# Perceiver layer with cross attention, heads and feed-forward: one block for the last two stages, and six fold pairs in two groups of three

## The chip, the cores and the metric

The kernel runs on one core of a Trainium2 chip. The metric is the device time of one execution in microseconds. Each kernel was run several times; the median counts, and one execution was also profiled.

## The reference

```python
x = x + _L0_xattn_ref(_layernorm(x), ctx_1024, gamma, beta, w_q, w_kv, w_out, b_out, gate)
x = x + _L0_attn_ref(_layernorm(x), W_Q, W_K, W_V)
x = x + _L0_ffn_ref(_layernorm(x), w_gate, w_up, w_down)
```

`x` is 64 x 32 x 512 (2048 tokens), the context 64 x 257 x 512, all float32. The cross attention normalises its input again with `gamma` and `beta`, has 16 heads of 64 elements, and gives `(out @ w_out + b_out) * tanh(gate)`. The second attention works inside each token: with Q, K, V split into 16 heads of 32 elements, K is softmaxed over the heads, Q over the elements, and the heads' products are mixed. The feed-forward has 1536 hidden elements, `silu(gate) * up`, and integer weights scaled by 1/127.

## The kernel before, in words

All large products are made three times over from a high and a low part of each operand (`three`, lines 80 to 84), with a moving side of 258 or 512 columns. The high parts come from ScalarE, the low parts (raw minus high) from VectorE or GpSimd.

There are three stages, each in a block of its own, so that each engine's program ends at the block's end and starts anew. `project_queries` writes the queries to memory. `cross_attention` works in 16 turns of four batches. `heads_and_mlp` makes output projection, second attention and feed-forward for 16 tiles of 128 tokens and then 4 turns of 512 tokens. Within a block the order of the instructions on each engine is written out by hand, and semaphores join the engines.

One turn of `cross_attention`, on TensorE: for each batch the probabilities are turned (`turn_probs`, line 574), the next batch is scored (`scores`), and the context is mixed by the probabilities in four chunks (`mix_chunk`, each 6 products). VectorE keeps each chunk (`keep_mix`, line 679). At the end of the turn `out_half` makes the heads' outputs in two halves (lines 600 and 607), ScalarE and VectorE split them into `x_o_hi` and `x_o_lo` (lines 794 and 701), and the sync queue stores them as `o_hi`, `o_lo` (line 423). Meanwhile the next turn's queries are folded with the key weights: `fold_pair` (line 540) makes eight matmuls of 64 rows for each of eight pairs of heads, ScalarE takes the high part (`high_fold`, line 780), VectorE the low part (`low_fold`, line 686). A pair uses two banks of PSUM (`FOLD_BANK`), and a pair that reuses banks waits until the earlier pair's low part is made (`FOLD_AFTER`): pair 3 for pair 0, pair 4 for pair 1, pair 5 for pair 2. VectorE's `keep_last` (lines 691 and 694) turns the last context row's probabilities; it waits for GpSimd's `last_ready`.

The last of the 16 turns is written out apart. It has no folds; instead the 20 pieces of the output and Q, K, V weights are loaded (`load_w`, line 434: 8 pieces of `w_out`, 4 each of `aq`, `ak`, `av`, 256 KB each), rounded by ScalarE (line 789) and split by GpSimd (even pieces) and VectorE (odd ones, `w_low`, line 394).

`heads_and_mlp` begins with four small loads and the loads of tiles 0 and 1 (`load`, lines 1061 and 1063: `a_oT_hi` and `a_oT_lo` of 512 KB each, `a_xin` of 256 KB), then six loads of feed-forward pieces (line 1089, 256 KB each). For each tile TensorE makes the output projection (24 products of `a_oT` with `w_out`, which lies in `w_cT` and the first part of `w_space`). VectorE adds gate, bias and input (`a_x`, line 1451) and takes moments and rows (`a_xn`, line 140, with GpSimd's power in between). TensorE turns them (line 1180), ScalarE and VectorE split them (`a_xT_hi`, `a_xT_lo`, lines 1326 and 1440), and then come the K, Q and V projections of 12 products each. A tile's output projection stands one tile ahead: that of tile 1 stands between tile 0's turning and its K projection.

Of the kernel before, what the change touches and what calls it, by code (L numbers as in the profile page):

```python
# [13 lines left out]

# [8 lines left out]
P = 128  # L23
# [299 lines left out]
def cross_attention(nc, hw, ahead, ctx_nat, ctx_T, last_T, q_dram, v_dram, o_hi, o_lo, identity, heads):  # L323
# [17 lines left out]
    with ExitStack() as ctx:  # L341
        s = Scope(nc, ctx, "x")
        wk, w_v, q, raw_n, raw_T = ahead.wk, ahead.w_v, ahead.q, ahead.raw_n, ahead.raw_T
        fold = hw.fold
        mix = s.sb("mix", [P, DC, GB, heads * SQ])
        cn = [s.pair(f"cn{i}", [P, KT, dim]) for i in range(2)]
        cT = hw.cT
        prob = s.sb("prob", [P, TILES, SKE])
        pT = [s.pair(f"pT{i}", [P, KT, heads * SQ]) for i in range(2)]
        last_p = s.sb("last_p", [P, TILES, GB, SQ])  # L350
        last_v = s.sb("last_v", [P, inner])
        last_z, last_t = s.sb("last_z", [P, TILES, SQ]), s.sb("last_t", [P, TILES, SQ])
# [24 lines left out]
        last_kept = s.count("last_kept", 1)
        mixed, mix_kept = s.count("mixed", GB * DC), s.count("mix_kept", GB * DC)
        o_ready = s.count("o_ready", 2, 2)
        o_hi_done, o_lo_done = s.count("o_hi_done", 2), s.count("o_lo_done", 2, 2)  # L380
        o_stored = s.count("o_stored", 64, 32)
        l_loaded, v_ready, v_copied, v_stored = s.sem("l_loaded"), s.sem("v_ready"), s.sem("v_copied"), s.sem("v_stored")
        all_last, lT = mix[0:B, 0, 0:2, :], mix[:, 1, 0, 0:DC * B].rearrange("p (c b) -> p c b", c=DC)
        slots = [wk[:, j, :] for j in range(PAIRS)]
        slots += [a[:, :, :].rearrange("p j n -> p (j n)")[:, h * dim:(h + 1) * dim] for a in (q, raw_T) for h in range(2)]
        RING, PIECES = len(slots), len(hw.pieces)
        w_loaded = [s.sem(f"w_loaded{i}") for i in range(RING)]
        w_hi_done, w_lo_done = s.sem("w_hi_done"), [s.sem("w_lo_pool"), s.sem("w_lo_dve")]
# [12 lines left out]
        @block.sync
        def _(sp):
            def load_T(t, b):
                sp.dma_start(raw_T[:, :, :], ctx_T[t * GB + b].rearrange("(c p) k -> p c k", p=P)).then_inc(T_loaded.sem, 16)

            def load_n(t, b):
                sp.dma_start(raw_n[:, :, :], ctx_nat[t * GB + b, 0:KT * P, :].rearrange("(k p) d -> p k d", p=P))\
                    .then_inc(n_loaded.sem, 16)

            def load_q(t, ahead):  # L410
                sp.dma_start(q[:, :, :], q_dram[:, :, bass.ds((t + ahead) * P, P)]).then_inc(q_loaded.sem, 16)

            def load_v(t):
                sp.wait_ge(o_ready.sem, o_ready.at(t, 0))
                for g in range(HT):
                    dst = last_v[g * SQ:g * SQ + GB, :].rearrange("b (i g e) -> b i g e", g=HT, e=HE)[:, :, g, :]
                    src = v_dram[bass.ds(t * GB, GB), :].rearrange("b (i g e) -> b i g e", g=HT, e=HE)[:, :, g, :]
                    sp.dma_start(dst, src).then_inc(v_loaded.sem, 16)

            def store_out(t, m):  # L420
                sp.wait_ge(o_lo_done.sem, o_lo_done.at(t, m + 1))
                for dst, src in zip((o_hi, o_lo), o):
                    sp.dma_start(dst[4 * m:4 * m + 4, :, bass.ds(t * P, P)].rearrange("j p n -> p j n"), f32(src[:, :, :]))\
                        .then_inc(o_stored.sem, 16)

            def load_w(numbers):
                for n in numbers:
                    if n == 0:
                        sp.wait_ge(fold_ready.sem, fold_ready.at(TURNS - 1, PAIRS))
                    if n == PAIRS + 2:  # L430
                        sp.wait_ge(Tlo_done.sem, Tlo_done.at(TURNS - 1, GB))
                    if n >= RING:
                        sp.wait_ge(w_lo_done[n % 2], (n - RING) // 2 + 1)
                    sp.dma_start(slots[n % RING], hw.pieces[n][0]).then_inc(w_loaded[n % RING], 16)

            def turn(t, more):
                load_v(t)
                if not more:
                    load_w(range(PAIRS + 2))
                if more:  # L440
                    sp.wait_ge(fold_ready.sem, fold_ready.at(t, PAIRS))
                    load_q(t, 1)
                for b in range(GB - 1):
                    if b + 2 < GB or more:
                        sp.wait_ge(nlo_done.sem, nlo_done.at(t, b + 2))
                        load_n(t, b + 2)
                    if more:
                        sp.wait_ge(Tlo_done.sem, Tlo_done.at(t, b + 4))
                        load_T(t, b + 4)
                if not more:  # L450
                    load_w(range(PAIRS + 2, RING + 4))
                store_out(t, 0)
                if more:
                    sp.wait_ge(nlo_done.sem, nlo_done.at(t, GB + 1))
                    load_n(t, GB + 1)
                    sp.wait_ge(Tlo_done.sem, Tlo_done.at(t, GB + 3))
                    load_T(t, GB + 3)
                else:
                    load_w(range(RING + 4, PIECES))
                store_out(t, 1)  # L460

            sp.dma_start(ident[:, :], identity).then_inc(once, 16)
            sp.dma_start(lT, last_T.rearrange("(c p) b -> p c b", p=P)).then_inc(l_loaded, 16)
            for done in (T_loaded, q_loaded, n_loaded):
                sp.sem_inc(done.sem, 16)  # L465
            for g in range(HT):
                sp.dma_start(own[g * SQ:(g + 1) * SQ, :], identity[0:SQ, 0:GB]).then_inc(once, 16)
            sp.wait_ge(cleared, 1)
            for b in range(2):
                sp.wait_ge(Tlo_done.sem, Tlo_done.at(0, b + 1))  # L470
                load_T(0, b + 1)
# [5 lines left out]
            with sp.Fori(0, TURNS - 1) as t:  # L477
                turn(t, True)
# [1175 lines left out]
```

## Time and profile before

| | |
|---|---|
| median of 3 runs | 1916.24 us (1915.59 to 1916.68) |
| the profiled execution, its own time | 1916.39 us |
| its span in the profile | 1914.6 us |
| TensorE matmul busy | 97% of the span |
| VectorE, ScalarE, GpSimd busy | 54%, 35%, 29% |
| mean granted clock of TensorE | 0.991 of 2.4 GHz |
| a turn of the cross attention | 66.87 us |
| start of the last cross turn, end of the cross attention on TensorE | about 1154 us, 1208.97 us |

The span begins with the first instruction of the program and ends with the last; the execution's own time has 1.8 us more around it. The profile names lines of the kernel, tiles by the names in the program (`x_` for the cross attention, `a_` for heads, `f` for feed-forward, `w_` and `e_` for what both share), and for each instruction what ended the idle time in front of it. PE is TensorE, PEld its weight loads, DVE VectorE, ACT ScalarE, POOL GpSimd, SPq the sync queue's issues.

### The profile page before, as it was taken

How to read it: one execution, taken by the hardware profiler on the slowest of the kernel's cores; microseconds unless marked ns; L12 is line 12 of the kernel's file. 1: busy time of each engine (PE TensorE's matmuls, PEld its weight loads, DVE VectorE, ACT ScalarE, POOL GpSimd, SP SyncE). 2: the span in 40 equal slices, each digit the busy share in tenths (PEclk: the TensorE clock that was granted, in tenths of full speed). 3: DMA queues.
4: the chain of work that ended last, by engine and by line, in shares of the span. 5: the costliest groups of instructions: out<-in, count | busy, mean ns of one | idle time of the engine just before them, and what ended most of it. 6: DMA issues, size and time to landing. Idle time of an engine off the chain costs nothing. (4 is left out here: it accounts for less than half of the span.)

```text
span 1914.6 us, 36622 instructions
## 1 busy us (share of the span) xinstructions
PE 1857.1 (97%) x14096; PEld 1607.2 (84%) x14096; DVE 1039.1 (54%) x2015; ACT 666.2 (35%) x1356; POOL 558.6 (29%) x546
## 2 busy tenths in 40 slices
PE   5989999999999999999999999599999999999999
PEld 4868988988998898899989888488888788888887
DVE  7614555455455545545554555388889763333322
ACT  3235444444444444444444445221111231111111
POOL 3015334433533444353344436231112000000000
PEclk9999999999999999999999999799999999999999
DMA  7323223322322332232233223633352131000000
GB/s 244 128 85 99 86 61 103 99 77 77 110 78 66 99 99 78 76 110 77 67 98 99 81 73 127 184 84 88 99 154 73 57 126 65 3 34 32 21 24 22
DMA packets 166629, 165.65 MB, mean 87 GB/s; under 512 B 8688, under 2 KB 123888, under 8 KB 166576
## 3 DMA queue, kind: packets, MB, share of 16 engines
q1 hardware_dynamic: 162144, 156.27, 27.1%
q10 hardware_dynamic: 4432, 8.65, 1.2%
q8 instruction: 36, 0.59, 0.1%
q14 instruction: 17, 0.14, 0.0%
HBM read 131.08 MB, written 33.82 MB: 86 GB/s over the span
## 5 line engine op out<-in xcount | busy, mean ns | idle before, releaser
L497 POOL TENSOR_TENSOR x_prob<-x_prob,x_share 128x256 f32<-128x256 f32 x256 | 157.0, 613 | 602.9 <-DVE x_share L662 595.7
L82 PE MATMUL x_ps<-w_cT_hi,w_space_hi 128*128 128x258 f32 x1024 | 296.1, 289 | 0.0
L83 PE MATMUL x_ps<-w_cT_lo,w_space_hi 128*128 128x258 f32 x1024 | 290.7, 284 | 0.0
L84 PE MATMUL x_ps<-w_cT_hi,w_space_lo 128*128 128x258 f32 x1024 | 288.5, 282 | 0.0
L679 DVE COPY x_mix<-x_ps 128x512 f32<-128x512 f32 x256 | 176.2, 688 | 115.1 <-PE x_ps L84 114.9
L82 PE MATMUL x_ps<-x_pT_hi,x_cn_hi 128*128 128x512 f32 x512 | 208.1, 406 | 1.5 <-DVE x_mix L679 1.5
L686 DVE TENSOR_TENSOR w_space_lo<-x_ps,w_space_hi 128x512 fp32r<-128x512 f32 x256 | 161.0, 680 | 78.4 <-ACT w_space_hi L780 45.8
L84 PE MATMUL x_ps<-x_pT_hi,x_cn_lo 128*128 128x512 f32 x512 | 201.2, 393 | 0.0
L769 ACT ACTIVATE x_prob<-x_ps,x_negmax 128x257 f32<-128x257 f32 x256 | 122.1, 477 | 227.1 <-DVE x_negmax L657 227.1
L83 PE MATMUL x_ps<-x_pT_lo,x_cn_hi 128*128 128x512 f32 x512 | 199.7, 390 | 0.0
L657 DVE TENSOR_REDUCE x_negmax<-x_ps 128x1 f32<-128x257 f32 x256 | 108.1, 422 | 166.2 <-PE x_ps L84 166.2
L82 PEld LDWEIGHTS x_ps<-w_cT_hi,w_space_hi 128*128 128x128 f32 x1024 | 193.8, 189 | 2.0 <-issue 0.2
L83 PEld LDWEIGHTS x_ps<-w_cT_lo,w_space_hi 128*128 128x128 f32 x1024 | 193.8, 189 | 0.0
L84 PEld LDWEIGHTS x_ps<-w_cT_hi,w_space_lo 128*128 128x128 f32 x1024 | 193.5, 189 | 0.0
L780 ACT ACTIVATE w_space_hi<-x_ps 128x512 fp32r<-128x512 f32 x256 | 132.4, 604 | 124.0 <-PE x_ps L540 124.0
L491 POOL TENSOR_TENSOR x_cn_lo<-e_raw_n,x_cn_hi 128x1024 fp32r<-128x1024 f32 x64 | 153.3, 2395 | 0.0
L540 PEld LDWEIGHTS x_ps<-e_q,e_wk 64*128 64x128 f32 x2048 | 122.2, 192 | 27.7 <-issue 18.7
L486 POOL TENSOR_TENSOR w_cT_lo<-e_raw_T,w_cT_hi 128x1028 fp32r<-128x1028 f32 x64 | 141.5, 2210 | 5.8 <-ACT w_cT_hi L757 5.8
L540 PE MATMUL x_ps<-e_q,e_wk 64*128 64x128 f32 x2048 | 134.4, 282 | 7.5 <-SPq L465 4.9
L600 PE MATMUL x_ps<-x_mix,e_wv 128*64 128x128 f32 x2048 | 138.3, 275 | 0.8 <-DVE x_mix L679 0.8
L600 PEld LDWEIGHTS x_ps<-x_mix,e_wv 128*64 128x64 f32 x2048 | 114.2, 137 | 12.3 <-issue 5.4
L82 PEld LDWEIGHTS x_ps<-x_pT_hi,x_cn_hi 128*128 128x128 f32 x512 | 96.1, 188 | 23.6 <-DVE x_mix L679 1.9
(205 smaller groups left out, 3546.6 us busy)
## 6 DMA issues: line engine op xcount, KB each, us to landing
e_raw_T<-ctx_T SPq DMA_DIRECT2D x64, 514.0 KB, 4.0
e_raw_n<-ctx_nat SPq DMA_DIRECT2D x64, 512.0 KB, 3.6
q<-q_q ACTq DMA_DIRECT2D x16, 512.0 KB, 2.8
e_q<-q SPq DMA_DIRECT2D x16, 512.0 KB, 4.2
o_hi<-x_o_hi SPq DMA_DIRECT2D x32, 256.0 KB, 2.4
o_lo<-x_o_lo SPq DMA_DIRECT2D x32, 256.0 KB, 3.0
a_oT_hi<-o_hi SPq DMA_DIRECT2D x16, 512.0 KB, 4.4
a_oT_lo<-o_lo SPq DMA_DIRECT2D x16, 512.0 KB, 5.6
```

Of the source, the lines that this page charges most:

```text
L82: pe.matmul(out, lhs[0], rhs[0], start=start, stop=False)
L83: pe.matmul(out, lhs[0], rhs[1], start=False, stop=False)
L84: return pe.matmul(out, lhs[1], rhs[0], start=False, stop=stop)
L486: pool.tensor_tensor(cT[b % 2][1][:, :, 0:SK], raw_T[:, :, :], f32(cT[b % 2][0][:, :, 0:SK]), ALU.subtract).then_inc(Tlo_done.sem, 1)
L491: pool.tensor_tensor(cn[b % 2][1][:, :, :], raw_n[:, :, :], f32(cn[b % 2][0][:, :, :]), ALU.subtract).then_inc(nlo_done.sem, 1)
L497: pool.tensor_tensor(prob[:, i, 0:KT * P], prob[:, i, 0:KT * P], share[:, i:i + 1].to_broadcast([P, KT * P]), ALU.mult)\
L540: mm = pe.matmul(ps[:, FOLD_BANK[j][h], c * P:(c + 1) * P], wk[r, j, c * P:(c + 1) * P], q[r, j, :], start=True, stop=True)
L600: pe.matmul(out[h], w_v[:, c, n * HE:(n + 1) * HE], mix[:, c, :, n * SQ:(n + 1) * SQ], start=c == 0, stop=False)
L679: dve.tensor_copy(mix[:, c, b, :], ps[:, M_BANK[c % 2], :]).then_inc(mix_kept.sem, 1)
L686: dve.tensor_tensor(lo, ps[:, FOLD_BANK[j][h], :].rearrange("p (c n) -> p c n", n=SQ), f32(hi), ALU.subtract).then_inc(fold_lo.sem, 1)
L769: act.activation(prob[:, i, 0:SK], ps[:, S_BANK[i], 0:SK], ACT.Exp, bias=negmax[:, i:i + 1], accum_out=total[:, i:i + 1]).then_inc(exp_don ...
L780: act.activation(of_head(fold[0], 2 * j + h), ps[:, FOLD_BANK[j][h], :].rearrange("p (c n) -> p c n", n=SQ), ACT.Copy)\
```

## The change

The last two stages become one block: `cross_attention` and `heads_and_mlp` return their programs for each engine, and `build` puts them one behind the other. PSUM and the identity are shared. The tiles of the heads are laid out anew, so that tile 0's and tile 1's inputs, bias, gate and mask can be loaded while the cross attention still runs. In the last cross turn the sync queue loads tile 0 after three quarters of the mixing, tile 1 after the pieces of `ak`, then mask, bias and gate; ScalarE's `tanh`, VectorE's gated bias and GpSimd's first two additions also move there. The output projection of tile 1 now stands ahead of tile 0's turning, in another bank (`DOTS`). GpSimd and VectorE each make two of the last weight splits later. The feed-forward's first loads wait for all weight splits. Tile 1's projection no longer stands ahead of K.

In the turns with folds, pairs 0 to 2 stand together ahead of the last batch's mixing, pairs 3 to 5 between its second and third chunk.

The core of the diff, without the changed indentation:

```diff
     def tensor(pe):
@@ turn
                 mix_chunk(t, 2, 2)
                 mix_chunk(t, 2, 3)
                 if more:
-                    fold_pair(t, 1, 0)
-                    fold_pair(t, 1, 1)
+                pe.wait_ge(pT_lo.sem, pT_lo.at(t, GB * KT))
+                for j in range(3):
+                    fold_pair(t, 1, j)
                 for c in range(DC):
                     mix_chunk(t, 3, c)
-                    if more and c % 2 == 0:
-                        fold_pair(t, 1, 2 + c)
-                        fold_pair(t, 1, 3 + c)
+                if more and c == 1:
+                    for j in range(3, 6):
+                        fold_pair(t, 1, j)
     def vector(dve, first_bias):
                 keep_mix(t, 2, 2)
-                if more:
-                    low_fold(t, 1, 0)
                 keep_mix(t, 2, 3)
                 if more:
+                low_fold(t, 1, 0)
                     low_fold(t, 1, 1)
                 for c in range(DC):
                     keep_mix(t, 3, c)
                     if c == 0:
                         keep_last(t)
-                    if more and c > 0:
-                        low_fold(t, 1, 1 + c)
+                if more and c < 2:
+                    low_fold(t, 1, 2 + c)
...
                 if more:
+                low_fold(t, 1, 4)
                     low_fold(t, 1, 5)
...
                 low_out(t, 1)
                 if not more:
-                    w_low(dve, range(15, PIECES, 2))
+                first_bias()
+                w_low(dve, (15,))
     def sync(sp, first_loads):
-                    load_w(range(PAIRS + 2, RING + 4))
+                load_w(range(PAIRS + 2, RING))
+                first_loads(0)
+                load_w(range(RING, RING + 4))
+                first_loads(1)
                 store_out(t, 0)
...
-            sp.wait_ge(o_stored.sem, 32 + TURNS * o_stored.per)
     def gpsimd(pool, first_bias):
-                    w_low(pool, range(0, PIECES, 2))
+                w_low(pool, range(0, 16, 2))
+                first_bias()
+                w_low(pool, range(16, PIECES, 2))
     def scalar(act, first_tanh):
                     w_high(range(RING, 16))
+                first_tanh()
                 high_out(t, 1)
...
+    def late_weights(dve):
+        w_low(dve, range(17, PIECES, 2))
@@ heads_and_mlp
+    def first_loads(sp, part):
+
+        c, last = cross, cross.last
+        if part == 0:
+            sp.wait_ge(c.mixed.sem, c.mixed.at(last, 3 * c.mixed.per // c.batches))
+            sp.wait_ge(c.turned.sem, c.turned.at(last, c.turned.per))
+            sp.wait_ge(c.last_ready.sem, c.last_ready.at(last, c.batches))
+        sp.wait_ge(c.o_stored.sem, c.o_stored.at(part + 1, 0))
+        load(sp, 0, part)
+        if part == 1:
+            sp.wait_ge(c.mixed.sem, c.mixed.at(last, c.mixed.per))
+            for dst, src in ((mask[:, :], same_token), (gated_bias[:, :], bias.partition_broadcast(P)),
+                             (gate_b[:, :], gate.partition_broadcast(P))):
+                sp.dma_start(dst, src).then_inc(once, 16)
...
@@ sync, step
+                if tile_of(t, i) == 0:
+                    sp.wait_ge(cross.o_stored.sem, cross.o_stored.at(cross.last + 1, 0))
+                load(sp, t, i + 2)
@@ sync, load_w of the feed-forward
                 for n in numbers:
+                if n == 0:
+                    for done in cross.w_lo_done:
+                        sp.wait_ge(done, len(hw.pieces) // 2)
...
+                if n == gate_up_at[1] + 4:
+                    sp.wait_ge(x2_stored[0].sem, x2_stored[0].at(TURNS, 0))
@@ gpsimd
+    def first_rows(pool):
+        pool.wait_ge(bias_done, 1)
+        add_bias(pool, 0, 0)
+        add_bias(pool, 0, 1)
@@ tensor, step
+            if tile_of(t, i) == 0:
+                add_out(t, 1, DOTS)
                 if there(t, i):
                     pe.wait_ge(normed.sem, normed.at(t, i + 1))
...
-                if there(t, i + 1):
+            if there(t, i + 1) and tile_of(t, i) != 0:
...
+                if tile_of(t, i) == 0:
+                    weights_done(16)
                     project(t, i, 1, K, k_ready)
...
+        def weights_done(pieces):
+            for done in cross.w_lo_done:
+                pe.wait_ge(done, pieces // 2)
...
-            pe.wait_ge(once, 64)
+        weights_done(PAIRS)
             all_steps(pe, step)
@@ vector, step
                     norm_scale(dve, xn, src, moments, rstd, 1).then_inc(normed.sem, 1)
+                if tile_of(t, n) == 0:
+                    cross.late_weights(dve)
```

GpSimd's program of the heads still begins with `pool.sem_inc(x2_done.sem, 4)`, the four credits for which VectorE waits ahead of each `a_x`; it now stands behind the last weight splits. The heads' tiles `a_oT`, `a_x`, `a_xin` have new places, and with them the feed-forward's `y`, `h` and their helpers.

How the instructions move is seen in three places. TensorE, at the end of a turn with folds; `e_q,e_wk` are the fold matmuls, `x_pT,x_cn` the mixing. Before, for the islands of pairs 2 and 3 and of pairs 4 and 5:

```order
L540 MATMUL x_ps<-e_q,e_wk 128x128 x16
...
L540 MATMUL x_ps<-e_q,e_wk 128x128 x8
L536 REGISTER_ALU
L540 MATMUL x_ps<-e_q,e_wk 128x128 x8
L82 MATMUL x_ps<-x_pT_hi,x_cn_hi 128x512
...
L536 REGISTER_ALU
L540 MATMUL x_ps<-e_q,e_wk 128x128 x8
```

Now, the first island of three and the second:

```order
L622 REGISTER_ALU
L532 REGISTER_ALU
L538 MATMUL s_ps<-e_q,e_wk 128x128 x24
L585 REGISTER_ALU
L83 MATMUL s_ps<-x_pT_hi,x_cn_hi 128x512
...
L534 REGISTER_ALU
L538 MATMUL s_ps<-e_q,e_wk 128x128 x8
L534 REGISTER_ALU
L538 MATMUL s_ps<-e_q,e_wk 128x128 x8
L534 REGISTER_ALU
L538 MATMUL s_ps<-e_q,e_wk 128x128 x8
```

Pairs 0 to 2 have one row of 24 matmuls, and pairs 3, 4 and 5 follow each other with a wait ahead of each.

The sync queue, from the last pieces of `aq` in the last cross turn. Before:

```order
L434 DMA e_raw_T<-aq 128x512 x2
L434 DMA e_wk<-ak 128x512 x4
L423 DMA o_hi<-x_o_hi 128x4x128
L423 DMA o_lo<-x_o_lo 128x4x128
L434 DMA e_wk<-av 128x512 x4
```

Now:

```order
L430 DMA e_raw_T<-aq 128x512 x2
L1082 DMA a_oT_hi<-o_hi 128x8x128
L1082 DMA a_oT_lo<-o_lo 128x8x128
L1084 DMA a_xin_1062<-x 128x512
L430 DMA e_wk<-ak 128x512 x4
...
L1084 DMA a_xin_1063<-x 128x512
L1077 DMA a_mask<-same_token 128x128
L1077 DMA a_bias<-b_out 128x512
L1077 DMA a_gate<-gate 128x1
L419 DMA o_hi<-x_o_hi 128x4x128
```

Tile 0's three loads stand ahead of `ak`, tile 1's and the small ones between `ak` and the first store.

GpSimd, from its last weight splits on. Before:

```order
L394 TENSOR_TENSOR w_space_lo<-e_wk,w_space_hi 128x512 x4
L341 UNCONDITIONAL_BRANCH
...
L1159 MEMSET a_power 128x4
L1127 TENSOR_TENSOR a_xin_3424<-a_xin_3424,a_bias 128x512
L1132 TENSOR_TENSOR a_rstd<-a_shifted,a_power 128x1
```

Now:

```order
L391 TENSOR_TENSOR w_space_lo<-e_wk,w_space_hi 128x512 x2
L1149 TENSOR_TENSOR a_xin_1062<-a_xin_1062,a_bias 128x512
L1149 TENSOR_TENSOR a_xin_1063<-a_xin_1063,a_bias 128x512
L391 TENSOR_TENSOR w_space_lo<-e_wk,w_space_hi 128x512 x2
L1187 MEMSET a_power 128x4
L1160 TENSOR_TENSOR a_rstd<-a_shifted,a_power 128x1 x2
```

Two additions stand between the splits, and the last two splits ahead of the first power.

## Rows read from the trace of the kernel before

**Rows 1.** The page: busy time, share of the span, instructions of each engine.

```profile
PE 1857.1 (97%) x14096; PEld 1607.2 (84%) x14096; DVE 1039.1 (54%) x2015; ACT 666.2 (35%) x1356; POOL 558.6 (29%) x546
```

**Rows 2.** Waits of TensorE, 1190 to 1300: engine line, released by, us, times, longest.

```profile
PE a_ps L82 <- DMA a_xin<-x: 15.6, 1, 15.6
PE a_ps L1180 <- DVE a_xn L140: 4.1, 1, 4.1
```

**Rows 3.** Windows: us, busy of PE, PEld, DVE, ACT, POOL, PEclk, DMA share, GB/s.

```profile
1194.00:1198.00 4.00, 2.53 (x11) 1.76 (x11) 3.96 (x5) 2.15 (x5) 4.00 (x4) 1.00 0.06 8
1226.00:1230.00 4.00, 4.00 (x12) 3.14 (x11) 0.00 (x0) 0.00 (x0) 0.00 (x0) 0.56 1.10 356
```

**Rows 4.** Timeline of TensorE at the boundary: start, us, operation, [idle before, releaser].

```profile
1208.58 0.39 PE L607 MATMUL x_ps<-x_last_p,x_last_v 128*64 128x128 f32 x4
1224.52 0.77 PE L82 MATMUL a_ps<-w_cT_hi,a_oT_hi 128*128 128x512 f32 x1 [15.55 <-DMA a_xin<-x]
...
1225.51 0.63 PE L84 MATMUL a_ps<-w_cT_hi,a_oT_lo 128*128 128x512 f32 x1
1225.94 0.63 PE L82 MATMUL a_ps<-w_cT_hi,a_oT_hi 128*128 128x512 f32 x1
...
1244.11 0.39 PE L82 MATMUL a_ps<-w_space_hi,a_xT_hi 128*128 128x512 f32 x1
...
1252.28 0.60 PE L1180 MATMUL a_ps<-a_ident,a_xn 128*128 128x128 f32 x4
```

**Rows 5.** Timeline of TensorE around two fold islands of the eighth turn.

```profile
589.48 0.40 PE L84 MATMUL x_ps<-x_pT_hi,x_cn_lo 128*128 128x512 f32 x1
589.81 2.06 PE L540 MATMUL x_ps<-e_q,e_wk 64*128 64x128 f32 x32
...
592.13 0.39 PE L83 MATMUL x_ps<-x_pT_lo,x_cn_hi 128*128 128x512 f32 x1
...
596.63 0.39 PE L84 MATMUL x_ps<-x_pT_hi,x_cn_lo 128*128 128x512 f32 x1
```

**Rows 6.** Timeline of VectorE in the same stretch.

```profile
587.67 1.29 DVE L674 TENSOR_TENSOR x_pT_lo<-x_ps,x_pT_hi 128x512 fp32r<-128x512 f32 x2 [0.70 <-ACT x_pT_hi L775]
...
594.64 0.68 DVE L679 COPY x_mix<-x_ps 128x512 f32<-128x512 f32 x1
...
595.67 0.69 DVE L694 TENSOR_TENSOR x_last_p<-x_last_t,x_own 128x512 f32<-128x512 f32 x1
597.06 0.69 DVE L679 COPY x_mix<-x_ps 128x512 f32<-128x512 f32 x1 [0.70 <-PE x_ps L84]
597.67 1.28 DVE L686 TENSOR_TENSOR w_space_lo<-x_ps,w_space_hi 128x512 fp32r<-128x512 f32 x2
```

**Rows 7.** Timeline of the sync queue's issues at the boundary.

```profile
1191.90 6.77 SPq L434 DMA_DIRECT2D e_wk<-ak  x4
...
1224.27 1.86 SPq L1089 DMA_DIRECT2D f_raw<-wg  x4
```

**Rows 8.** DMA issues of 1185 to 1240: KB each, median us to landing.

```profile
a_xin<-x SPq DMA_DIRECT2D x3, 256.0 KB, 6.3
```

**Rows 9.** Timeline of VectorE and GpSimd at the boundary.

```profile
1210.84 0.68 DVE L394 TENSOR_TENSOR w_space_lo<-e_wk,w_space_hi 128x512 fp32r<-128x512 f32 x1
1211.22 3.10 POOL L394 TENSOR_TENSOR w_space_lo<-e_wk,w_space_hi 128x512 fp32r<-128x512 f32 x2 [2.41 <-ACT w_space_hi L789]
...
1220.62 0.48 DVE L1569 TENSOR_SCALAR a_bias<-a_bias,a_tanh 128x512 f32<-128x512 f32 x1 [5.76 <-ACT a_tanh L1386]
...
1224.55 1.27 POOL L1127 TENSOR_TENSOR a_xin<-a_xin,a_bias 128x512 f32<-128x512 f32 x1 [9.06 <-DMA a_xin<-x]
...
1232.58 0.75 DVE L1451 SCALAR_TENSOR_TENSOR a_x<-a_ps,a_tanh,a_xin 128x512 f32<-128x512 f32 x1 [11.47 <-PE a_ps L84]
...
1235.14 1.48 DVE L140 TENSOR_SCALAR a_xn<-a_x,a_moments,a_rstd 128x512 f32<-128x512 f32 x1 [0.67 <-POOL a_rstd L1132]
...
1253.54 0.69 DVE L1440 TENSOR_TENSOR a_xT_lo<-a_ps,a_xT_hi 128x512 fp32r<-128x512 f32 x1 [0.35 <-ACT a_xT_hi L1326]
```

More of the change, by code:

```diff
@@ L13 @@
 from contextlib import ExitStack
+from dataclasses import dataclass
 import concourse.bass as bass
@@ new lines, in cross_attention @@
+    s = Scope(nc, ctx, "x")
+    wk, w_v, q, raw_n, raw_T = ahead.wk, ahead.w_v, ahead.q, ahead.raw_n, ahead.raw_T
+    fold = hw.fold
+    mix = s.sb("mix", [P, DC, GB, heads * SQ])
+    cn = [s.pair(f"cn{i}", [P, KT, dim]) for i in range(2)]
+    cT = hw.cT
+    prob = s.sb("prob", [P, TILES, SKE])
+    pT = [s.pair(f"pT{i}", [P, KT, heads * SQ]) for i in range(2)]
+    last_p = s.sb("last_p", [P, TILES, GB, SQ])
+    last_v = s.sb("last_v", [P, inner])
+    last_z, last_t = s.sb("last_z", [P, TILES, SQ]), s.sb("last_t", [P, TILES, SQ])
@@ L912, in pair, with heads_and_mlp @@
         return self.sb(name + "_hi", shape, F32R), self.sb(name + "_lo", shape, F32R)
-def heads_and_mlp(nc, ahead, hw, x, bias, gate, o_hi, o_lo, x2, identity, same_token, wg, wu, wd, out, scale):
+def heads_and_mlp(nc, ctx, ps, ident, start, cross, ahead, hw, x, bias, gate, o_hi, o_lo, x2, identity, same_token, wg, wu, wd, out, scale):
     tokens, dim = x.shape
@@ new lines, in heads_and_mlp @@
+    x2o = [area.sb("x2o0", [P, dim])]
+    over = area.at
+    oT = [None, area.pair("oT1", [P, PAIRS, P])]
+    on_oT = [Area(nc, "f1", over), None]
+    on_y = Area(nc, "fy", area.at)
+    x1 = [area.sb(f"x1{i}", [P, dim]) for i in range(4)]
+    xin = [area.sb(f"xin{i}", [P, dim]) for i in range(2)]
+    area.at += 64
+    on_oT[1] = Area(nc, "f0", area.at)
+    oT[0] = area.pair("oT0", [P, PAIRS, P])
+    gated_bias = area.sb("bias", [P, dim])
+    x2o.append(area.sb("x2o1", [P, dim]))
+    mask = area.sb("mask", [P, P])
@@ new lines, in heads_and_mlp, with gate_up_pieces @@
+    w_g.append(on_rows.pair("wg2", [P, DC, dim]))
+    w_u.append(on_rows.pair("wu2", [P, DC, dim]))
+    assert on_rows.at == over and HC == 12 and CHUNKS == 3
+    wsrc = [w.rearrange("(c p) n -> c p n", p=P) for w in (wg, wu, wd)]
+    pieces, gate_up_at, down_at = [], [], []
+    def gate_up_pieces(n):
+        for src, dst in ((wsrc[0], w_g), (wsrc[1], w_u)):
+            pieces.extend((src[c, :, n * dim:(n + 1) * dim], dst[n][0][:, c, :], dst[n][1][:, c, :]) for c in range(DC))
+        gate_up_at.append(len(pieces))
```

2035 lines of the change are left out of this document (1018 added, 1017 removed).

## The prediction

> **What bounds the kernel now.** I read the page first. TensorE is busy for 1857.1 of 1914.6 us [rows 1], so a change can only pay where TensorE waits or where its stream has dead steps. The waits of TensorE around the end of the cross attention come next [rows 2]: 15.6 us until the first tile's `a_xin` has landed, and 4.1 us until its normalised rows `a_xn` exist. The windows [rows 3] give the clock: 1.00 of full speed (2.4 GHz) in the last cross turn, but 0.56 at 1226 to 1230, where the first products of the heads run after the long wait; a good part of that window is at the lower level (1.2 GHz). The timeline places this [rows 4]: the last product of the cross attention begins its group at 1208.58 and is over at 1208.97, the first head product begins at 1224.52, the K projection of tile 0 at 1244.11. Everything from 1208.97 to 1244.11 is 35.1 us for 48 output products and four transposes.
>
> What a product costs at full clock is in the same rows: K, Q and V of tile 0 are 36 products between 1244.11 and 1252.28, so 0.227 us each. 48 of them are 10.9 us.
>
> The second place is the fold islands. In every turn but the last, eight pairs of 64-row products (`L540`) stand between groups of other products. The timeline of one of them [rows 5]: the last product before an island starts at 589.48, the island at 589.81, and the second product after it at 592.13, 2.65 us in all. The 16 matmuls in it (32 records) take 2.06 - 0.27 = 1.79 us from first to last start, 0.112 each, and two ordinary steps of 0.23 make 0.46. The remaining **0.40 us** is what entering and leaving one island costs.
>
> **The change, part by part.**
>
> *Islands.* Pairs 0 to 5 stood in three islands of two, now in two of three; pairs 6 and 7 stay. One entry and exit less in 15 turns (the last turn has no folds): 15 x 0.40 = **6.0 us less**, if no new wait appears. Two could. (a) The new wait for `pT_lo` before pair 0: its work on VectorE begins at 587.67 and lasts 1.29 us [rows 6], over at 588.96; the island begins at 589.81 [rows 5]. 0.85 us to spare, cost nothing. (b) Pair 5 waits for VectorE's subtractions of pair 2, and these now stand behind `keep_mix(3,0)` and `keep_last`. Count from the first island's start. The last matmul of three pairs starts at 24 x 0.112 = 2.68, the second product behind an island 0.53 later (592.13 against 589.81 + 1.79), the sixth four steps of 0.23 later, at 4.14, and the copy follows 0.43 later, as 597.06 follows 596.63 [rows 5, 6]: 4.57. From that copy to `x_last_p` are 1.03 us (594.64 to 595.67), the next instruction can start 0.60 behind it, and the two subtractions take 1.28 [rows 6]: done at 7.48. TensorE comes to pair 5 at 4.14 + 6 x 0.23 + 0.32 + 16 x 0.112 + 0.1 = 7.73, and loads its weights about 0.1 earlier. About 0.1 us to spare. Price zero, bound from above one VectorE step (0.60) in each turn.
>
> *The boundary.* Both blocks become one, so no branch, no barrier and no wait for the last stores stand between them. The loads of tile 0 and tile 1 move ahead of the weights `ak` and of the last stores on the sync queue. Tile 0 goes out after three quarters of the last turn's mixing, about 1191.8, just ahead of the four `ak` loads that now begin at 1191.90 [rows 7]; a load behind two others takes 6.3 us to land [rows 8], so it is there near 1199, ten microseconds early. Tile 1 goes out after the `ak` loads, whose issues end at 1191.90 + 6.77 = 1198.67 [rows 7]; two more issues, and 6.3 us: near 1206. Two tiles are 2.5 MB, in a stretch of which the queue spent most waiting for VectorE. Behind them stand mask, bias and gate, which by the same count land near 1208, and the first store. ScalarE's `tanh` waits for the gate ahead of the second `x_o_hi`, and so does VectorE's slot at 1210.84 behind the second `x_o_lo` [rows 9]: 2.8 us to spare, less ScalarE's and VectorE's own 1.3. I take zero, bound 1 us, since the chain below starts there.
>
> TensorE then goes from 1208.97 straight into 48 products: 10.9 us and about 0.4 for the step between kinds, done at 1220.3. Beside it runs the chain to tile 0's rows. VectorE's slot is at 1210.84, and the bias takes 0.48 there: 1211.32. GpSimd adds it to two tiles at 1.27 each: 1213.86. It then makes two more weight splits of the same size (I take 1.27 each, as for the addition), and only after them hands out the four credits for which VectorE's first `a_x` waits: 1216.4. From `a_x` to the end of `a_xn` took 1235.14 + 1.48 - 1232.58 = 4.04 us: 1220.5 [rows 9]. So the transposes start at 1220.5 or 1220.6, both sides equal. Before, the second 24 products covered the time from the transposes to K; now they are used up. Transposes, ScalarE's copy and VectorE's difference took 1253.54 + 0.69 - 1252.28 = 1.95 us, with the release 2.0 [rows 4, 9]: **this wait is new, some 1.7 us of idle TensorE**. K starts at 1222.6 where it started at 1244.11: **21.5 us less**. Ends of this term: 1220.3 + 2.0, if GpSimd is earlier, gives 21.8; with the slower splits (3.10 for two [rows 9]) it is 20.9.
>
> On the two splits the Trainium skill (SBUF — State Buffer, the rule on the shared port pair) says that a VectorE instruction with two SBUF inputs and a GpSimd instruction that reads SBUF exclude each other, the later one blocking fully. By that rule the VectorE split that now follows the bias at 1211.4 meets GpSimd's first addition, which would begin some 0.7 us later, and the K projection with it: 20.8 instead of 21.5, a sum of 1890.5. It lies inside the ends just named (20.9 within 0.1).
>
> *What is late next.* The six feed-forward loads moved behind the last of the weight splits, the two that VectorE makes after `a_xn`: 1220.5 + 1.3 = 1221.8. Six issues at 1.86 / 4 are 2.8 us, then come the three loads of tile 2, whose last goes out about 1.2 later and lands 6.3 us after that [rows 7, 8]: 1232.1. TensorE wants it 8.2 + 0.3 us after K's start: 1231.1. **1.0 us of new wait**; I take 0.9. Ends: 0 if the loads run without gaps, 2.5 if ScalarE's first feed-forward pieces and GpSimd's third addition, both now late, push more.
>
> Sum, against the profiled execution's own 1916.39 (span 1914.6): -21.5 - 6.0 + 0.9 = -26.6, **1889.8 us**. The median of the runs shown is 0.15 lower than that execution, which I leave.
>
> **The rivals.**
> 1. *Pair 5 stops every turn.* For it speaks the margin of 0.1 us, against it that the trace's VectorE steps repeat to 10 ns. If VectorE is one step of 0.60 late, 0.5 us are lost 15 times: 1889.8 + 7.5 = 1897.3. Chance 0.10.
> 2. *The boundary keeps part of its gap.* A chain that is late (gate, GpSimd, tile 2) by 3 us in all, for instance: 1893. Nor is the lower clock excluded: TensorE idles about 1.7 us before K. In 1194 to 1198 TensorE was busy for 2.53 of 4.00 us and the clock stayed at 1.00 [rows 3], while products at 1225.51 and 1225.94, behind the wait of 15.6 us, are 0.43 apart [rows 4]. If it fell, I count 12 products at 0.43 instead of 0.227, as many as the window at 0.56 holds: 2.4 us more, 1892. [...] Chance of this rival 0.15.
> 3. *It ends slower.* The mechanism would be the island of three: `keep_last` waits for GpSimd's `x_last_z`, and now holds back pair 2's subtractions and so pair 5. If it made TensorE wait more than 26.6 / 15 = 1.8 us a turn beyond what the island saves, the kernel would be slower; at 2.2 us it is 1896 + 27, some 1923. Against it: VectorE went from that copy to `x_last_p` in 1.03 us without a wait [rows 6]. Chance 0.03.
> 4. *It does not do what it says:* tile 0 is held by the mixing or by the stores, and the gap stays, leaving the 6 us of the folds: 1910. Chance 0.02.
>
> **How the numbers follow.** The forecast has 0.70. Its own range is 1887.5 (margins better than worked out, no wait for tile 2) to 1892. Rival 2 adds up to 1894.5; what is left out above is rival 1, 3 and 4 with some 0.15. So 1887.5 to 1894.5. A measurement can tell about 0.2% (3.8 us) from no change; the first two cases and the forecast lie beyond it: faster 0.95, same 0.02, slower 0.03.
>
> **What would show it.** Right: the wait for `a_xin` of 15.6 us gone, K of tile 0 within 14 us of the last cross product, a wait of 1.5 to 2 us ahead of it that ends with `a_xT_lo`, one of about 1 us for tile 2's load, the clock at 1.00 throughout, and turns that are 0.40 us shorter, with no wait inside the islands. Wrong: a wait on `w_space_lo` in each turn (rival 1), products 0.43 us apart after the boundary, or a wait for `a_xin` of more than 3 us.

## The result and the profile after

The changed kernel took 1898.82 us (median of 4 runs, 1897.20 to 1899.87), the kernel before beside it on the same chip 1916.46 (1915.59 to 1919.39, 4 runs). The ratio is 0.9905, 95% interval 0.9887 to 0.9922. It is faster, by 17.6 us instead of the 26.6 that the sum gave, and outside the range of 1887.5 to 1894.5.

The profiled execution took 1897.99 us, its span is 1896.2. The row of the engines hardly differs from [rows 1]; TensorE is busy 98% of the span where it was 97%:

```profile
PE 1857.4 (98%) x14096; PEld 1604.4 (85%) x14096; DVE 1039.5 (55%) x2015; ACT 664.8 (35%) x1356; POOL 559.2 (29%) x546
```

**The boundary came as summed.** TensorE's waits between 1180 and 1300, which answer to [rows 2]; the columns are the same:

```profile
PE s_ps L83 <- DVE x_mix L677: 1.5, 1, 1.5
PE s_ps L83 <- DVE a_xT_lo L1481: 1.4, 1, 1.4
PE s_ps L598 <- DVE x_mix L677: 0.8, 1, 0.8
PE s_ps L83 <- DMA a_xin<-x: 0.4, 1, 0.4
```

Its timeline there, which answers to [rows 4]:

```profile
1201.75 0.39 PE L605 MATMUL s_ps<-x_last_p,x_last_v 128*64 128x128 f32 x4
1202.07 0.50 PE L83 MATMUL s_ps<-w_cT_hi,a_oT_hi 128*128 128x512 f32 x1
...
1215.30 0.50 PE L83 MATMUL s_ps<-w_space_hi,a_xT_hi 128*128 128x512 f32 x1 [1.41 <-DVE a_xT_lo L1481]
...
1223.60 0.60 PE L1207 MATMUL s_ps<-s_ident,a_xn 128*128 128x128 f32 x4
1224.56 0.47 PE L83 MATMUL s_ps<-w_cT_hi,a_oT_hi 128*128 128x512 f32 x1 [0.36 <-DMA a_xin<-x]
```

The waits of 15.6 and 4.1 us are gone; the two that end with `x_mix` stood in the kernel before as well, with the same lengths. From the last cross product to K of tile 0 it is 13.5 us (1201.75 to 1215.30), with one wait for `a_xT_lo` in it, and tile 2's load costs 0.4. K begins 28.81 us earlier than it did (1244.11, [rows 4]).

**The islands came as summed, too.** TensorE's timeline in the eighth turn, which answers to [rows 5]:

```profile
586.73 0.40 PE L85 MATMUL s_ps<-x_pT_hi,x_cn_lo 128*128 128x512 f32 x1
587.05 2.95 PE L538 MATMUL s_ps<-e_q,e_wk 64*128 64x128 f32 x48
589.93 0.50 PE L83 MATMUL s_ps<-x_pT_hi,x_cn_hi 128*128 128x512 f32 x1
...
592.57 0.39 PE L85 MATMUL s_ps<-x_pT_hi,x_cn_lo 128*128 128x512 f32 x1
592.89 2.95 PE L538 MATMUL s_ps<-e_q,e_wk 64*128 64x128 f32 x48
```

Both islands hold three pairs (48 records), and neither they nor the products behind them show a wait in brackets. The second one is as long as the first (2.95 us), so nothing stopped between its pairs either. From one turn's first product with `x_last_p` to the next it is 66.41 us where it was 66.85 (mean of 14 turns each).

**What was gained is lost again in the feed-forward.** The first row transposes of its second and third turn, before:

```profile
1608.62 0.60 PE L1251 MATMUL a_ps<-a_ident,a_m_xn 128*128 128x128 f32 x4
...
1708.59 0.49 PE L1251 MATMUL a_ps<-a_ident,a_m_xn 128*128 128x128 f32 x3
```

and after:

```profile
1582.93 0.60 PE L1287 MATMUL s_ps<-s_ident,a_m_xn 128*128 128x128 f32 x4
...
1685.30 0.60 PE L1287 MATMUL s_ps<-s_ident,a_m_xn 128*128 128x128 f32 x4
```

A turn takes 102.37 us instead of 99.97. The lead of the changed kernel is 27.6 us when the feed-forward starts (1498.6 against 1471.1, unrounded), 25.7 after its first turn, 23.3 and 20.9 after the next two, 18.4 at the end: **9.2 us go there**. No wait does it. Windows of one such turn (us; busy and count of PE, PEld, DVE, ACT, POOL; clock; DMA share; GB/s), before:

```profile
1608.00:1708.00 100.00, 100.00 (x450) 82.78 (x449) 34.46 (x59) 16.95 (x28) 1.01 (x1) 1.00 0.09 32
```

and after:

```profile
1583.00:1685.00 102.00, 102.00 (x448) 82.53 (x447) 34.52 (x58) 16.94 (x28) 1.01 (x1) 1.00 0.09 31
```

TensorE is busy throughout, at the same clock of 1.00 (2.4 GHz), beside the same work of the other engines and the same DMA traffic, and still needs 2% longer for as many products. Groups of the same products by shape (name, count, busy us, mean ns of one record), before:

```profile
L82 PE MATMUL a_ps<-a_m_xT_hi,f_wg_hi 128*128 128x512 f32 x16 | 6.3, 396 | 0.0
L83 PE MATMUL a_ps<-a_m_xT_lo,fhi_wg 128*128 128x512 f32 x16 | 6.2, 389 | 0.0
L84 PE MATMUL a_ps<-a_m_xT_hi,flo_wg 128*128 128x512 f32 x16 | 6.2, 389 | 0.0
L82 PE MATMUL a_ps<-ft_wd_hi,fo_h_hi 128*128 128x512 f32 x16 | 6.2, 390 | 0.0
```

and after:

```profile
L83 PE MATMUL s_ps<-a_m_xT_hi,f_wg_hi 128*128 128x512 f32 x16 | 6.4, 399 | 0.0
L84 PE MATMUL s_ps<-a_m_xT_lo,fhi_wg 128*128 128x512 f32 x16 | 6.3, 395 | 0.0
L85 PE MATMUL s_ps<-a_m_xT_hi,flo_wg 128*128 128x512 f32 x16 | 6.3, 395 | 0.0
L83 PE MATMUL s_ps<-ft_wd_hi,f_h_hi 128*128 128x512 f32 x16 | 6.3, 395 | 0.0
```

Every group is 3 to 6 ns longer. A record overlaps its neighbours, so the pace is better read from the starts. Ten products further it is 2.27 us before:

```profile
1649.65 0.39 PE L83 MATMUL a_ps<-ft_wd_lo,fo_h_hi 128*128 128x512 f32 x1
...
1651.92 0.39 PE L84 MATMUL a_ps<-a_m_xT_hi,flo_wg 128*128 128x512 f32 x1
```

and 2.32 us after:

```profile
1623.62 0.39 PE L85 MATMUL s_ps<-a_m_xT_hi,flo_wu 128*128 128x512 f32 x1
...
1625.94 0.39 PE L83 MATMUL s_ps<-ft_wd_hi,f_h_hi 128*128 128x512 f32 x1
```

Over the last two turns (intervals of 218 to 250 ns between two starts, nearly 900 of them) the products stood 226.7 to 229.0 ns apart before and 232.6 to 233.1 after, by group. On average that is 5.6 ns, and 432 products of a turn by 5.6 ns are 2.4 us, the whole loss.

What differs? The instructions are the same in the same order. Some operands have moved: `m_xT`, the moving operand of gate and up (512 columns), `h`, the stationary operand of down, and the weights `wg2` and `wu2`, these by 24064 bytes, which is a multiple of 256. The weights are stationary in gate and up and moving in down. The first bytes in a partition, and the remainder by 256:

| tile | before | after |
|---|---|---|
| `m_xT` (hi) | 211392, 192 | 211776, 64 |
| `h` (first, hi) | 141760, 192 | 189440, 0 |
| `wg0`, `wu0` | 8320, 128 (`wg0`) | the same |
| other `wg`, `wu`, all `wd` | 192 | 192 |

Before, all but `wg0` and `wu0` stood at 192, and the products with just these two were the slower ones, at 229.0. That is the theory of the experiments: **a product's pace hangs on where its two operands lie.** The rival is the merged program: instructions that lie elsewhere, or something that the other engines do beside. Paces below are means by group over the last two feed-forward turns of the profiled execution; with another choice of intervals they move by up to 0.4 ns.

### The profile page after: what moved, and what is told of

Read it like the earlier page. It is cut to its first block, busy times and chain, and to the rows that moved or that the text cites. A ratio compares the mean times of both kernels' runs of the same rounds, so it can differ in the third digit from the quotient of the medians.

```text
span 1896.2 us, 36612 instructions
## 1 busy us (share of the span) xinstructions
PE 1857.4 (98%) x14096; PEld 1604.4 (85%) x14096; DVE 1039.5 (55%) x2015; ACT 664.8 (35%) x1356; POOL 559.2 (29%) x546
## 4 chain that ended last, share of the span: by engine, by line
PE 90%; DVE 1%; DMA 1%; SPq 1%; POOL 0%; issue 0%; ACT 0%; ACTq 0%; DVEq 0%; POOLq 0%
PE s_ps L83 24%; PE s_ps L84 23%; PE s_ps L85 23%; PE s_ps L538 7%; PE s_ps L598 6%; PE s_ps L572 3%; PE s_ps L605 1%; PE s_ps L1265 1%; PE s_ps L1276 1%; PE s_ps L1207 0%; DMA a_xin<-x 0%; DMA a_m_xn<-x 0%; PE s_ps L1287 0%; PE s_ps L546 0%; PE s_ps L1256 0%
## 5 line engine op out<-in xcount | busy, mean ns | idle before, releaser
L83 PE MATMUL s_ps<-w_cT_hi,w_space_hi 128*128 128x258 f32 x1024 | 295.9, 289 | 0.0
L84 PE MATMUL s_ps<-w_cT_lo,w_space_hi 128*128 128x258 f32 x1024 | 290.5, 284 | 0.0
L85 PE MATMUL s_ps<-w_cT_hi,w_space_lo 128*128 128x258 f32 x1024 | 288.4, 282 | 0.0
L677 DVE COPY x_mix<-s_ps 128x512 f32<-128x512 f32 x256 | 176.7, 690 | 121.7 <-PE s_ps L85 121.7
L83 PE MATMUL s_ps<-x_pT_hi,x_cn_hi 128*128 128x512 f32 x512 | 206.4, 403 | 1.5 <-DVE x_mix L677 1.5
L767 ACT ACTIVATE x_prob<-s_ps,x_negmax 128x257 f32<-128x257 f32 x256 | 122.2, 477 | 226.7 <-DVE x_negmax L655 226.6
L85 PE MATMUL s_ps<-x_pT_hi,x_cn_lo 128*128 128x512 f32 x512 | 201.0, 393 | 0.0
L84 PE MATMUL s_ps<-x_pT_lo,x_cn_hi 128*128 128x512 f32 x512 | 199.8, 390 | 0.0
L83 PEld LDWEIGHTS s_ps<-w_cT_hi,w_space_hi 128*128 128x128 f32 x1024 | 193.7, 189 | 2.0 <-issue 0.2
L84 PEld LDWEIGHTS s_ps<-w_cT_lo,w_space_hi 128*128 128x128 f32 x1024 | 193.9, 189 | 0.0
L85 PEld LDWEIGHTS s_ps<-w_cT_hi,w_space_lo 128*128 128x128 f32 x1024 | 193.3, 189 | 0.0
```

Of the source, the lines that this page charges most:

```text
L83: pe.matmul(out, lhs[0], rhs[0], start=start, stop=False)
L84: pe.matmul(out, lhs[0], rhs[1], start=False, stop=False)
L85: return pe.matmul(out, lhs[1], rhs[0], start=False, stop=stop)
L677: dve.tensor_copy(mix[:, c, b, :], ps[:, M_BANK[c % 2], :]).then_inc(mix_kept.sem, 1)
L767: act.activation(prob[:, i, 0:SK], ps[:, S_BANK[i], 0:SK], ACT.Exp, bias=negmax[:, i:i + 1], accum_out=total[:, i:i + 1]).then_inc(exp_don ...
```

## The experiments

Each number beside a label is a median of 4 to 5 runs; the kernel before took 1918.40, 1917.82 and 1917.66 us beside the three groups of runs.

**1. Both operands back to 192, nothing else.**

```diff
-    on_oT[1] = Area(nc, "f0", area.at)
+    on_oT[1] = Area(nc, "f0", area.at + 192)
-    m_xn, m_xT = area.sb("m_xn", [P, TT, dim]), area.pair("m_xT", [P, DC, N])
+    m_xn = area.sb("m_xn", [P, TT, dim])
+    area.at += 128
+    m_xT = area.pair("m_xT", [P, DC, N])
```

> The changed kernel with two tiles moved and no instruction changed: m_xT 128 bytes further (its offset within 256 bytes is 192 again, as in the kernel before) and the pair h 192 bytes further (192 again). Theory 'places': the products of the feed-forward became slower because of where their operands lie. Then the products go from 232.8 ns apart back to 227, a feed-forward turn from 102.4 to 100.0 us, and the time falls by about 9 us to 1889.5. Rival 'program': the slower products come from the merged block (where the instructions lie and how they are fetched), or from something that ACT, DVE or the queues do beside them; then a turn stays at 102.4 us and the time at 1898.8.

1890.19 us, ratio 0.9855 (0.9839 to 0.9872). One feed-forward turn and one group of it:

```profile
1582.00:1682.00 100.00, 100.00 (x451) 82.87 (x450) 34.52 (x58) 16.98 (x29) 1.01 (x1) 1.00 0.10 32
```

```profile
L84 PE MATMUL s_ps<-a_m_xT_lo,fhi_wg 128*128 128x512 f32 x16 | 6.2, 389 | 0.0
```

The turn is back at 99.95 us, the pace at 226.7 (229.0 with `wg0` and `wu0`). The rival falls: the merged block with the same instructions is as fast as the old one.

**2. Each of the two alone.** Only the second half of the edit, then only the first.

> The changed kernel with m_xT alone 128 bytes further. Places: the gate and up products (288 of the 432 of a turn, 6.3 ns each for two thirds of them and 4 ns for the third with wg0 and wu0) get back to their old pace, the down products stay at 232.6 ns: 6.4 us less than the changed kernel, 1892.4. Program: 1898.8.

1893.69 us, a turn 101.07 us, gate and up at 227.7, down at 233.2.

> The changed kernel with the pair h alone 192 bytes further. Places: the down products (144 of a turn, 5.8 ns each, four turns) get back to 226.8 ns, gate and up stay slow: 3.3 us less than the changed kernel, 1895.5. Program: 1898.8.

1897.09 us, a turn 101.79 us, gate and up at 233.0, down at 228.5. From 102.37 the two take 1.30 and 0.58 us off a turn, together 1.88 of 2.42: the last half microsecond comes only with both, since a group whose operands are well placed is slower beside slow groups than in experiment 1 (228.5 and 227.7 instead of 226.9 and 226.7). The expectations left that out: they had 1.6 and 0.8 us less a turn, 1.30 and 0.58 came. In four turns this is 1.2 and 1.0 us of the 1.3 and 1.6 by which the two times lie above them.

**3. The same displacement in the kernel before,** whose `m_xT` then stands at 64.

```diff
-        m_xn, m_xT = area.sb("m_xn", [P, TT, dim]), area.pair("m_xT", [P, DC, N])
+        m_xn = area.sb("m_xn", [P, TT, dim])
+        area.at += 128
+        m_xT = area.pair("m_xT", [P, DC, N])
```

> The kernel before with m_xT 128 bytes further, so that its offset within 256 bytes is 64, as in the changed kernel; nothing else. Places: gate and up products go from 227 to 233 ns, a turn from 100.0 to 101.6 us, the time to 1922.9 (6.4 us more). Program: no change, 1916.5.

1924.80 us, 6.4 us above the kernel before (ratio 1.0035, 1.0021 to 1.0049), a turn 101.84 us (101.6 expected), gate and up at 233.0, and down, which has both its operands where they were, at 228.8 instead of 226.9. One displaced operand makes the old program slower, with no change in its instructions.

**4. Distance, or one good place?** Experiment 1 with other numbers:

```diff
-    on_oT[1] = Area(nc, "f0", area.at + 192)
+    on_oT[1] = Area(nc, "f0", area.at + 64)
-    area.at += 128
+    area.at += 64
```

> The changed kernel with m_xT 64 and h 64 bytes further. Offsets within 256 bytes are now 128 for m_xT (the operand that moves through in gate and up), 128 for wg0 and wu0, 192 for the other gate and up weights; 64 for h (the stationary operand of down) against 192 for wd. Theory 'distance' (what counts is the stationary operand's offset less that of the moving one: 0 gave 226.7 ns, 192 gave 229.0, 64 and 128 gave 232.6 to 233.2): products with wg0 and wu0 at 226.7 ns, all other gate and up ones at 233, down at 233; time 1890.2 - 0.9 + 4.8 + 3.4 = 1897.5. Rival 'one good place' (an operand is fast at offset 192 and slow elsewhere, each by itself): products with wg0 and wu0 stay at 229 or slower, 233 for the rest; time 1898.8 or more.

1895.94 us, 1.6 below the expectation; the time alone would not tell the two theories apart, the groups do. Three groups of its feed-forward:

```profile
L84 PE MATMUL s_ps<-a_m_xT_lo,fhi_wg 128*128 128x512 f32 x16 | 6.3, 394 | 0.0
L85 PE MATMUL s_ps<-a_m_xT_hi,fr_wg_lo 128*128 128x512 f32 x16 | 6.3, 394 | 0.0
...
L84 PE MATMUL s_ps<-a_m_xT_lo,f_wg_hi 128*128 128x512 f32 x16 | 6.2, 389 | 0.0
```

The order has turned round: `wg0` at 128, which was the slower one wherever the others were fast, is now the fast one (227.7 ns apart), since `m_xT` stands at 128 as well; those at 192 take 233.2, down 232.0.

Then `area.at += 192` ahead of `m_xT` and `area.at + 128` for `h`, which puts `m_xT` at 0 and `h` at 128:

> The changed kernel with m_xT 192 and h 128 bytes further: offsets 0 for m_xT, 128 for h. Distance: wg0 and wu0 are 128 away (233 ns), the other gate and up weights 192 away (229 ns), h against wd 192 away (229 ns); time 1890.2 + 1.6 + 1.8 + 1.2 = 1894.8. One good place: nothing but slow products, 1898.8.

1894.22 us: `wg0` and `wu0` 232.4, the other gate and up 229.6, down 229.7. So it is the distance, the stationary operand's place less that of the moving one. The feed-forward products of these runs together:

| distance in 256 bytes | ns from start to start | from |
|---|---|---|
| 0 | 226.7 to 227.0; 227.7 to 228.8 beside slow groups | before, experiments 1 to 5 |
| 64 | 232.6 to 233.2 | after (`wg0`, `wu0`, down), experiment 4 (other gate and up) |
| 128 | 232.0 to 233.0 | after (other gate and up), experiment 4 (down; `wg0`, `wu0`) |
| 192 | 229.0 to 229.7 | before, experiment 4 |

The period is not more than 256: 211392 and 61632 (`wg1`) are an odd multiple of 256 apart and fast. Distances that are no multiple of 64 were not tried, and why the distance matters stays open.

**5. The same for the rest.** Experiment 1, and:

```diff
+    on_ahead.at += 64
     w_g, w_u = [on_ahead.pair("wg0", [P, DC, dim])], [on_ahead.pair("wu0", [P, DC, dim])]
```

> places_both with wg0, wu0 and the six raw tiles behind them 64 bytes further too, so that wg0 and wu0 stand at 192 as m_xT does. Distance: their 96 products a turn go from 229.0 to 226.7 ns, four turns: 0.9 us less than places_both, 1889.3. If what is left at 229 ns has another cause: 1890.2.

1889.07 us; `wg0` and `wu0` at 226.9, a turn 99.72. The 0.23 us a turn are there, 0.9 in all.

Then also the mixing of the cross attention and `oT0` (the line ahead of `m_xT` becomes 192, and `h` lies where `oT0` does):

```diff
+    s.sb("gap", [P, 48])
     pT = [s.pair(f"pT{i}", [P, KT, heads * SQ]) for i in range(2)]
...
-    area.at += 64
+    area.at += 256
     on_oT[1] = Area(nc, "f0", area.at)
```

> both_and_wg0, and a gap of 192 bytes ahead of the cross attention's pT (with everything behind it in the cross attention) and ahead of oT0, so that pT stands at 192 as cn does, and oT0 as the wo pieces that lie in the space tiles. Distance: the 1536 products of pT and cn go from 229 to 226.7 ns (3.5 us in all) and those of oT0 in eight of the heads' tiles from 232.6 towards 227 (about 1.1 us): 1884.7. If the cross attention's turns do not follow their products (a wait takes the gain), 1888.

1887.51 us, ratio 0.9844 (0.9830 to 0.9857): **faster than both kernels**, and than the changed one by 11 to 12 us (0.9844 against 0.9905, each beside the kernel before). But 1.6 us less than the one before it, not 4.6. The mixing products went from 229.7 to 228.7 on average, not to 226.7, and a cross turn from 66.41 to 66.33. The 258-column products with `w_cT`, whose distances are mixed, stood 119 to 122 ns apart in every kernel.

The starts in the traces show where the mixing gained and where it didn't. In a run of mixing products with no other kind between them, those from the twelfth on went from 229.0 to 226.8 ns, as expected of distances 192 and 0; the first eleven, behind products of another kind, only from 230.1 to 229.5, and they are seven in ten. Nine products further, late in such a run of 24, in the changed kernel (2.06 us):

```profile
571.12 0.39 PE L83 MATMUL s_ps<-x_pT_hi,x_cn_hi 128*128 128x512 f32 x1
...
573.18 0.39 PE L83 MATMUL s_ps<-x_pT_hi,x_cn_hi 128*128 128x512 f32 x1
```

and with all in the same place (2.04 us):

```profile
571.42 0.39 PE L84 MATMUL s_ps<-x_pT_lo,x_cn_hi 128*128 128x512 f32 x1
...
573.46 0.39 PE L84 MATMUL s_ps<-x_pT_lo,x_cn_hi 128*128 128x512 f32 x1
```

The heads' output products on the pieces in the space tiles show the same: with `oT0`, which the change had moved from 192 to 0, they stood 233.0 ns apart, and about 230.3 after this experiment; with `oT1`, which stands at 192 in every kernel, 230.2 throughout. So the distance counts in these two stages too, but a second thing, which no run isolates, holds them at 229.5 and 230.2 there.

**6. The two parts by themselves.** The new islands in the kernel before, with the wait for `pT_lo` and VectorE's order of the change:

```diff
                 if more:
-                    fold_pair(t, 1, 0)
-                    fold_pair(t, 1, 1)
+                    pe.wait_ge(pT_lo.sem, pT_lo.at(t, GB * KT))
+                    for j in range(3):
+                        fold_pair(t, 1, j)
                 for c in range(DC):
                     mix_chunk(t, 3, c)
-                    if more and c % 2 == 0:
-                        fold_pair(t, 1, 2 + c)
-                        fold_pair(t, 1, 3 + c)
+                    if more and c == 1:
+                        for j in range(3, 6):
+                            fold_pair(t, 1, j)
```

> The kernel before with the islands of the changed kernel and nothing else (matmul order, the wait for pT_lo, the order of the low folds on VectorE). The turn of the changed kernel is 66.43 us against 66.87: 0.44 us in 15 turns, 6.6 us less than the kernel before, 1911.2. If the shorter turn hangs on anything else in the changed kernel: 1917.8.

1909.51 us, ratio 0.9960 (0.9946 to 0.9974), a turn 66.42 us. The same edit backwards in experiment 1, the boundary alone:

> places_both with the old islands: the boundary's part alone, with the old pace of the products. If the two parts are independent: 1890.2 + 6.6 = 1896.8, which is 20.9 us less than the kernel before.

1896.07 us, ratio 0.9883, a turn 66.83. By the times the islands are worth 5.9 to 8.2 us (6.6 by the turns), the boundary 21.6: together the 28 us of experiment 1.

**7. One block, but the loads late.** Experiment 1, and:

```diff
             store_out(t, 1)
+            if not more:
+                first_loads(2)
+                first_loads(3)
...
-        sp.wait_ge(c.o_stored.sem, c.o_stored.at(part + 1, 0))
-        load(sp, 0, part)
+        if part >= 2:
+            sp.wait_ge(c.o_stored.sem, c.o_stored.at(part - 1, 0))
+            load(sp, 0, part - 2)
```

> places_both, but SyncE issues the loads of the first two tiles (oT and xin) after the last turn's second store rather than ahead of the first; one block stays, mask, bias and gate stay early. Theory 'loads': what the boundary gained is the wait of 15.6 us for these loads; they are now issued at about 1205.5 and land 6.3 us later, where the first product on them stands at 1202: some 10 us more than places_both, 1900. Rival 'block': the end of the first block (all engines meeting, late start of the second) was the price, and the loads would be hidden anyway: 1890 to 1892.

1901.66 us, 11.5 above experiment 1. TensorE's waits, 1180 to 1300:

```profile
PE s_ps L83 <- DMA a_xin<-x: 10.0, 1, 10.0
...
PE s_ps L83 <- DVE a_xT_lo L1487: 1.4, 1, 1.4
```

Windows behind that wait, which ended at 1213.03:

```profile
1213.00:1217.00 4.00, 3.97 (x9) 3.14 (x10) 0.00 (x0) 0.00 (x0) 1.28 (x1) 0.50 0.94 251
1217.00:1221.00 4.00, 4.00 (x17) 3.25 (x16) 0.00 (x0) 0.00 (x0) 3.82 (x4) 0.90 0.01 4
```

About half of the boundary's 21.6 us is the wait for the loads, and the lower clock follows it: 9 products in 4 us at 0.50 (1.2 GHz) instead of 17 and more. From the first product to K are 15.4 us here, 13.2 in the changed kernel: 2.1 us. The other half goes with the rest of the edit at the boundary (one block, the bias and the first rows made earlier) and was not split further.

## Where the prediction was right and where it failed

- *Islands, 6.0 us.* Right. The turn is 0.44 us shorter instead of 0.40, 6.6 in 15 turns. No wait for `pT_lo` and none of pair 5, whose margin was reckoned at 0.1 us: rival 1 did not come. The count behind that margin holds: pair 2's subtractions end at 594.55, 7.50 us after the first island's start (587.05), and 7.48 had been reckoned.

```profile
593.27 1.28 DVE L684 TENSOR_TENSOR w_space_lo<-s_ps,w_space_hi 128x512 fp32r<-128x512 f32 x2
```

- *Boundary, 21.5 us.* Right. The kernel was 6.8 us ahead when the last turn's output products began (1200.94 against 1194.11), K 28.8: 22.0 at the boundary. The wait ended by `a_xT_lo` is 1.4 us, not 1.7.
- *The four credits.* That step was wrong, but the sum hardly hung on it: by the prediction's own count TensorE's 48 products ended only 0.2 us before that chain. `a_x` was to wait until GpSimd had made two more splits, but began beside them:

```profile
1207.96 0.75 DVE L1492 SCALAR_TENSOR_TENSOR a_x<-s_ps,a_tanh,a_xin 128x512 f32<-128x512 f32 x1 [2.47 <-PE s_ps L85]
```

```profile
1207.85 2.54 POOL L391 TENSOR_TENSOR w_space_lo<-e_wk,w_space_hi 128x512 fp32r<-128x512 f32 x2
```

  `a_xn` was done at 1211.71 and TensorE came to its transposes at 1213.29, so the 48 products set K.
- *GpSimd against VectorE.* The Trainium skill (SBUF — State Buffer, the rule on the shared port pair) would have put the sum 0.7 us higher. GpSimd's first addition is recorded from 1204.97 on, beside a VectorE split that ran from 1204.80 to 1205.49. The two additions took 2.92 us together, against 1.27 for one [rows 9]: 0.4 us more, where a full block until the split's end would be 0.5. The trace agrees with the rule within 0.1 us, and the delay was too small to reach K.
- *The clock.* No drop after the wait of 1.4 us. The window around it:

```profile
1213.00:1217.00 4.00, 2.59 (x13) 1.94 (x13) 2.34 (x6) 1.88 (x4) 0.00 (x0) 1.00 0.74 212
```

  Rival 2 did not come. By the Trainium skill (TensorE: Matmul & The Clock Gate, the part on loop nests) a TensorE that waits long for a DMA between products goes cold. The wait of 10.0 us in experiment 7 agrees (0.50 behind it); the one of 1.4 us, which is for VectorE, left the clock at 1.00.
- *Tile 2's load, 0.9 us.* 0.4 measured.
- **The failed step is the sum itself.** It ended at the boundary and carried its 26.6 us unchanged through the heads and the feed-forward. That the feed-forward's `h` and its helpers have new places stood in the description of the change, and `m_xT` had moved with them, but the prediction costed neither: not at nothing with a reason, but not at all. The missing term is +9.2 us in the feed-forward. With the places put right the same program took 1890.2, against the 1889.8 of the sum. That 1889.8 + 9.2 also meets the measured 1898.8 is in part luck: the lead at the start of the feed-forward was 27.6 us, 1.0 more than the sum had. None of the rivals had the term, and the range had no room for it. The signs that the prediction named all lie at the boundary and in the islands; they came, nearly to the number, while the time missed.
- *In the heads,* too, `oT0` had moved, and that was not costed either. If all 24 products of its 8 tiles lost the 2.8 ns of experiment 5, that is 0.5 us (an estimate).

## What to carry to other kernels

Where a change moves tiles, ask of each matmul operand that moved where it now starts against its partner, and look at the pace of the same products after: a stage that is all TensorE pays a few nanoseconds for each of its products, and neither a wait nor the clock shows it. In a layout written by offsets, 128 and 192 bytes of padding that make stationary and moving operand equal in 256 bytes were worth about 9 us here, a third of what the whole change was to bring. Products that stand between those of other kinds gained less. And a sum that ends where the change ends is only a part of the forecast: one row of each later stage that shares its tiles belongs in it.

## What the runs showed of the hardware

- The pace of the feed-forward's 128-row, 512-column fp32r products depends on the distance of the operands' start bytes within 256: 226.7 ns at 0, 229.0 to 229.7 at 192, 232.0 to 233.2 at 64 and 128. Mixing products late in a run follow it (229.0 at 192, 226.8 at 0); the first eleven of a run (229.5 at 0) and the heads' output products (233.0 at 64, 230.2 at 0) only in part. The record of a product is 389 ns long at 0 and 394 or 395 when slow; the weight loads on PEld take 188 ns in both.
- In the changed kernel's gate and up the starts alternate, 229 and 238 ns apart, product by product. A well-placed group beside slow ones is 1.0 to 1.9 ns slower than among its like (experiments 2 and 3).
- Semaphore credits that an engine gives without an instruction of its own did not wait for the two splits that it was still working on (1207.96 against 1210.39).
- Behind a wait of 10.0 us TensorE's granted clock was 0.50 (1.2 GHz) for 4 us and 0.90 for the next 4, and K came 2.1 us later after the first product; a wait of 1.4 us left it at 1.00.
